# Eight of sixteen scan inputs made ahead on GpSimd, and one product with C per step on VectorE

## The chip, the cores and the metric

The kernel runs on one core of one Trainium2 chip. A time is the device time of one execution in microseconds (us). The profile names the engines PE (TensorE matmul), PEld (TensorE weight load), DVE (VectorE), ACT (ScalarE), POOL (GpSimd) and SP (SyncE, which here only issues DMAs).

## The reference, cut to what matters

Two layers follow each other. The part that matters is the state-space branch of the first layer's attention block: batch 2, length L = 1024, D = 128 channels, N = 128 states.

```python
xp = xn @ Wx                                   # xn: normed x
dr, Bs, Cs = xp[..., :R], xp[..., R:R + N], xp[..., R + N:]
delta = softplus(dr @ Wdt + bdt)               # dt
xn = xn * sel * gate                           # two sigmoid gates
Bs, Cs = Bs * imp, Cs * imp
def step(h, inputs):
    dt, bt, ct, xt = inputs
    dA = exp(dt[:, :, None] * A)
    h = dA * h + dt[:, :, None] * bt[:, None, :] * xt[:, :, None]
    y = sum(h * ct[:, None, :], axis=-1)
    return h, y
```

Beside it runs a softmax attention (16 heads of size 8, 4 key heads) on the same x; both are added, and an expert layer, a latent attention and a second expert layer follow.

## The kernel before, in words

The work stands in stages, each an `nc.Block` that all engines leave together.

`prepare` (0 to 66 us) makes dt (`delta`), B and C (`bt`, `ct`, states by time), and `gate`, which in the end holds dt times x. TensorE turns `bt` and `gate` so that time lies across partitions (`b_turned`, `x_turned`), and ScalarE copies them out. dt times x is also split into three bfloat16 parts (`parts`): `rest` and `low` on VectorE, casts on ScalarE. SP writes `delta`, `bt`, `ct` and the three parts to memory.

`hybrid_attention` (66 to 542 us) is the softmax attention: `HybridFront` first, then 16 half units. VectorE takes the maxima of scores in a pair of PSUM banks (L556); when a half unit's maxima are there it makes their parts in five small operations (L567 to L571). GpSimd meanwhile makes inputs of the later scan ahead of time (`gpsimd_third`, L734): B turned times one column of dt times x, 128x1024, and sends it to memory by a DMA of its own queue (L737), with two buffers. It takes six such products for each half unit, and waits for the half unit's `mparts_ready` before the next six. SP's `sync_third` reloads `ct`, `bt` and the parts near the end.

`scan_states` (542 to 1168 us) runs the recurrence for one channel at a time with the 128 states on partitions. A unit is one channel and one batch element, 128 states by 1024 times; 16 units make a step, 8 steps (jj) a batch element, and there are two of these (b): 256 units. For a unit n of a step:

- SP loads the channel's row of dt, broadcast to 128 partitions (`dt`, L1434, 512 KB), into one of four buffers; ScalarE makes the decay exp(dt A) from it (`da`, L1555).
- The input dt B x has to be in a PSUM pair. There are three ways. TURNED (units 0, 2, 4 to 14): ScalarE multiplies eight 128x128 tiles (`ut`, L1563) and TensorE transposes them (L1456). AHEAD_UNITS (3, 5, 7, 11, 13, 15): SP loads what GpSimd made (`ua`, L1432, three buffers) and TensorE transposes it (L1464). SPREAD (1 and 9): two matmuls of the bfloat16 parts spread dt times x to all partitions (L1470), and VectorE multiplies it with `bt` (L1590).
- VectorE runs the scan (L1598) from `da` in SBUF and the pair in PSUM into `st`; GpSimd multiplies `st` with `ct` into `hc` (L1639, two SBUF inputs); TensorE sums `hc` over the states with a one-column matmul (L1480, `reduce`) for four units at a time, when the fourth product is there.

There are three PSUM pairs for inputs, so the fill of unit n waits for the scan of an earlier unit (n - 3 for most), and four buffers each of `dt`, `da` and `st`. TensorE's order is written out by hand:

```python
for n in range(UNITS):
    if n % 2 == 1:
        jp, h = n // 4 - 1, (n % 4) // 2
        ...                      # reduce(b, jj, jp, h)
    if n + AHEAD < UNITS:
        fill(b, jj, n + AHEAD)   # AHEAD = 2
```

So at n = 9 TensorE first sums units 4 to 7, which needs the product of unit 7 (`hc_ready`), and only then fills unit 11. The same holds at n = 5, 13 and 1 for units 3, 11 and 15 of the four before.

In the text below a scan of unit n is Sn, a product of `st` with `ct` is Pn.

## Time and profile before

| | |
|---|---|
| median of 3 runs | 2047.4 us (2046.13 to 2053.39) |
| the profiled execution | 2043.78 us, span 2042.0 us |
| busy over the span | PE 86%, DVE 72%, ACT 65%, POOL 43% |
| granted TensorE clock, mean | 0.912 |
| prepare, attention, scan | to 65.7, to 542.4, to 1167.9 us (L1493 ends there) |
| the costliest groups | L1639 POOL 599.1 us, L1598 DVE 562.2 us, both in the scan |

Share of busy time is an average over stages with different limits; for this change the prepare, attention and scan stages are to be read apart. In a timeline row consecutive instructions of one line are merged: the first number is the start, the second the time to the end of the last of them, and xcount how many there are. In brackets stands the idle time ahead of it and what ended it.

### The profile page before, as it was taken

What the parts mean: (1) busy time and instruction counts of PE and PEld (TensorE: products, weight loads), DVE (VectorE), ACT (ScalarE), POOL (GpSimd) and SP (SyncE); (2) the same over time, 40 slices, a digit from 0 to 9 for tenths busy, and PEclk for the clock granted to TensorE, in tenths of its full rate; (3) what the DMA queues carried; (4) which work ended last, traced back from release to release, by engine and by line L of the source; (5) the groups of instructions that cost most, each with busy time, mean ns of one, the idle gap of its engine ahead of it and who ended that gap; (6) DMA issues with size and microseconds to landing.
All of it is one profiled execution on the core that took longest, in us unless ns stands there. A gap on an engine that the chain in (4) does not pass through costs nothing. (4 is left out here: it accounts for less than half of the span.)

```text
span 2042.0 us, 32184 instructions
## 1 busy us (share of the span) xinstructions
PE 1760.0 (86%) x10624; PEld 756.7 (37%) x10624; DVE 1467.8 (72%) x1473; ACT 1323.3 (65%) x2673; POOL 886.7 (43%) x567
## 2 busy tenths in 40 slices
PE   7769999999887776777777799899999998999996
PEld 2312333333344444444444333334444443233332
DVE  3677888887299999999999754556666624455456
ACT  4426777777799999989999534335555553554343
POOL 1075565565299999999999710000000001000000
PEclk8758999999998888988888899859999987999998
DMA  2354444442699888879888411322223000000000
GB/s 108 136 174 149 151 162 160 151 151 115 197 322 316 303 305 310 308 274 307 300 313 300 154 67 43 66 56 51 46 44 59 19 18 0 0 0 0 0 6 16
DMA packets 86546, 288.88 MB, mean 141 GB/s; under 512 B 11671, under 2 KB 15026, under 8 KB 84383
## 3 DMA queue, kind: packets, MB, share of 16 engines
q1 hardware_dynamic: 72319, 236.57, 36.4%
q0 software_dynamic: 13824, 50.34, 6.5%
q8 instruction: 71, 1.16, 0.2%
q10 hardware_dynamic: 288, 0.45, 0.1%
q14 instruction: 44, 0.36, 0.1%
HBM read 214.60 MB, written 61.21 MB: 135 GB/s over the span
## 5 line engine op out<-in xcount | busy, mean ns | idle before, releaser
L556 DVE TENSOR_REDUCE attn_mx<-banks 128x1 f32<-128x1024 f32 (+7 forms) x512 | 501.6, 989 | 156.2 <-PE banks L363 99.1
L1639 POOL TENSOR_TENSOR hc<-st,ct 128x1024 f32<-128x1024 f32 x256 | 599.1, 2387 | 6.0 <-DVE st L1598 5.6
L1598 DVE TENSOR_TENSOR_SCAN st<-da,banks 128x1024 f32<-128x1024 f32 x256 | 562.2, 2265 | 15.8 <-ACT da L1555 5.6
L508 ACT ACTIVATE attn_probs<-banks 128x512 f32<-128x512 f32 (+3 forms) x640 | 307.4, 533 | 199.0 <-PE banks L397 102.2
L1563 ACT ACTIVATE ut<-b_turned,mats 128x128 f32<-128x128 f32 x1024 | 311.7, 387 | 1.7
L1555 ACT ACTIVATE da<-dt,mats 128x1024 f32<-128x1024 f32 x256 | 282.3, 1138 | 25.4 <-DVE st L1598 21.3
L393 PE MATMUL banks<-attn_qa,attn_ka 75*128 75x512 bf16 (+3 forms) x896 | 272.5, 373 | 3.9 <-DMA attn_qa<-attn_mrow 2.0
L1480 PE MATMUL banks<-hc,onecol 128*32 128x512 f32 x1024 | 160.0, 701 | 105.3 <-POOL onecol L1637 77.2
L734 POOL TENSOR_TENSOR made_ahead<-b_turned,x_turned 128x1024 f32<-128x1024 f32 x96 | 183.9, 1915 | 116.8 <-DVE attn_mparts L571 74.4
L361 PE MATMUL banks<-attn_ka,attn_qa 64*128 64x512 bf16 (+3 forms) x512 | 199.7, 391 | 34.2 <-DVE attn_mx L556 26.5
L413 PE MATMUL banks<-attn_probs,attn_vst 128*32 128x256 f32 (+3 forms) x2560 | 191.1, 369 | 1.7 <-ACT attn_osb L499 1.4
L1456 PE MATMUL banks<-mats,ut 128*128 128x128 f32 x1024 | 165.6, 301 | 30.5 <-DVE st L1598 19.8
L508 ACT ACTIVATE centred_squares<-banks 128x512 f32<-128x512 f32 x256 | 138.9, 594 | 62.5 <-PE banks L393 61.1
L1456 PEld LDWEIGHTS banks<-mats,ut 128*128 128x128 f32 x1024 | 134.7, 153 | 64.5 <-ACT ut L1563 35.1
L2574 PE MATMUL banks<-hid_m,ew 128*128 128x512 f32 x320 | 157.4, 627 | 0.0
L3011 POOL CAST route_ident<-mats 128x128 bf16<-128x128 f32 x1 | 0.3, 292 | 345.6 <-issue 345.6
L361 PE MATMUL banks<-attn_ku,attn_qu 64*128 64x512 bf16 (+3 forms) x384 | 145.7, 380 | 0.0
L1464 PEld LDWEIGHTS banks<-mats,ua 128*128 128x128 f32 x768 | 105.8, 169 | 107.1 <-issue 71.5
L1464 PE MATMUL banks<-mats,ua 128*128 128x128 f32 x768 | 132.2, 328 | 6.5 <-DVE st L1598 6.4
L393 PEld LDWEIGHTS banks<-attn_qa,attn_ka 75*128 75x128 bf16 x896 | 80.8, 98 | 132.6 <-issue 48.5
L361 PEld LDWEIGHTS banks<-attn_ka,attn_qa 64*128 64x128 bf16 x512 | 47.9, 94 | 207.0 <-issue 126.8
L413 PE MATMUL banks<-centred_squares,attn_vst 128*32 128x256 f32 x1024 | 83.1, 396 | 2.2 <-ACT attn_osb L499 2.2
(438 smaller groups left out, 1949.0 us busy)
## 6 DMA issues: line engine op xcount, KB each, us to landing
dt<-dt_rows SPq DMA_DIRECT2D x256, 512.0 KB, 5.6
ahead<-made_ahead POOLq DMA_DIRECT2D x96, 512.0 KB, 3.1
ua<-ahead SPq DMA_DIRECT2D x96, 512.0 KB, 5.8
attn_qa<-q_lin SPq DMA_DIRECT2D x144, 64.0 KB
attn_qu<-attn_qa SPq DMA_DIRECT2D x16, 512.0 KB, 4.3
attn_ka<-k_lin SPq DMA_DIRECT2D x72, 64.0 KB
moe_w<-in_moe_w SPq DMA_DIRECT2D x2, 2048.0 KB, 10.2
mats<-in_mats SPq DMA_DIRECT2D x1, 2876.5 KB, 12.9
```

What stands on the lines that cost most here:

```text
L361: ins = nc.tensor.matmul(out[:, lo:hi], lhs, rhs, start=True, stop=not diag)
L393: ins = nc.tensor.matmul(out[:, c0:BLK], ka[i % RING][0:KROWS, kj(j), sl(kt, TILE)], qa[i % RING][0:KROWS, j, qb * BLK + c0:(qb + 1) * BLK ...
L413: last = nc.tensor.matmul(out_acc[32 * j:32 * j + 32, cols], vstage[:, kt, kj(j), :], probs[(kt_slot + j // 2) % 4][:, j % 2, cols],  star ...
L508: nc.scalar.activation(probs[s % 4][:, jj, c0:BLK], scores_exp[jj][:, c0:BLK], ACT.Exp, scale=scale).then_inc(probs_ready, 1)
L556: nc.vector.reduce_max(mx[:, qt, j:j + 1], scores_max[n % 2][:, 0:w], AX.X)\
L734: nc.gpsimd.tensor_tensor(stage[:, :, :], scan.b_turned[:, 8 * b:8 * b + 8, :], x, ALU.mult)\
L1456: ins = nc.tensor.transpose(pair[:, i // 4, sl(i % 4, TILE)], buf[:, i, :], k.m("ident"))
L1464: ins = nc.tensor.transpose(pair[:, i // 4, sl(i % 4, TILE)], ua[q % 3][:, i, :], k.m("ident"))
L1555: nc.scalar.activation(da[n % 4][:, :], dt[n % 4][:, :], ACT.Exp, scale=a_now[:, g, jp:jp + 1])\
L1563: nc.scalar.activation(ut[TURNED.index(n) % 2][:, i, :], b_turned[:, 8 * b + i, :], ACT.Copy, scale=x_now[:, i, g, jp:jp + 1]).then_inc(ut ...
L1598: nc.vector.tensor_tensor_scan(st[n % 4][:, :], da[n % 4][:, :], pair[:, :, :].rearrange("p h t -> p (h t)"), 0.0, ALU.mult, ALU.add).then ...
L1639: nc.gpsimd.tensor_tensor(hc[n % 8][:, :], st[n % 4][:, :], ct[:, b * SEQ:(b + 1) * SEQ], ALU.mult)\
```

## The change

It makes five edits.

1. `AHEAD_UNITS` has eight units (2, 4, 6, 8, 10, 12, 14, 15) where it had six. GpSimd makes 128 products ahead where it made 96, eight for each half unit of the attention. `ua` has four buffers where it had three.
2. SPREAD is gone. TURNED is 0, 1, 3, 5, 7, 9, 11, 13, still eight units. VectorE makes no input any more.
3. The product of `st` with `ct` for unit 8 of each step goes from GpSimd to VectorE (`ON_DVE`); VectorE waits for its own scan and for `summed`, then multiplies. GpSimd passes over the unit.
4. With the spread its parts fall away: `rest`, `low`, eight casts, the `sel` table, and the writes and reloads of `bt` and the parts (one write of 1024 KB and three of 512 KB; one load of 1024 KB and twelve of 128 KB).
5. `bt` lives only until the end of the attention; the attention's own bfloat16 parts of q and k, which used the scan's `xparts` buffer, get one of their own.

```diff
         self.rs_tok = k.sb("rs_tok", [128, NT], ctx=ctx)
-        self.qparts = [scan.xparts[:, i, :] for i in range(3)]
-        self.kparts = [scan.xparts[:, 3, sl(i)] for i in range(3)]
+        parts = k.sb("qk_parts", [128, 4, T], BF16, ctx)
+        self.qparts = [parts[:, i, :] for i in range(3)]
+        self.kparts = [parts[:, 3, sl(i)] for i in range(3)]
         self.stage = [k.sb(f"made_ahead{i}", [128, SEQ // TILE, TILE], ctx=ctx) for i in range(2)]
...
         sp.dma_start(self.scan.ct[:, :], self.d["ct_kept"]).then_inc(self.scan_in, 16)
-        sp.dma_start(self.scan.bt[:, :], self.d["bt_kept"]).then_inc(self.scan_in, 16)
-        for p in range(3):
-            for g in range(4):
-                sp.dma_start(self.scan.xparts[32 * p:32 * p + 32, g, :], self.d["xparts_kept"][p, sl(g, 32), :])\
-                    .then_inc(self.scan_in, 16)
-        sp.wait_ge(self.scan_in, 16 * 14)
+        sp.wait_ge(self.scan_in, 16)
...
                 for m in AHEAD_UNITS:
-                    if n >= 7 and n % 6 == 1:
-                        pool.wait_ge(self.mparts_ready[(n // 6 - 1) % 2], (n // 6 + 1) // 2)
+                    if n >= 9 and n % 8 == 1:
+                        pool.wait_ge(self.mparts_ready[(n // 8 - 1) % 2], (n // 8 + 1) // 2)
                     channel = 32 * (m % 4) + 4 * jj + m // 4
...
         self.kept = kept
-        self.bt = k.sb("bt", [128, T], ctx=ctx)
         self.ct = k.sb("ct", [128, T], ctx=ctx)
         self.b_turned = k.sb("b_turned", [128, NT, 128], ctx=ctx)
         self.x_turned = k.sb("x_turned", [128, NT, 128], ctx=ctx)
-        self.xparts = k.sb("xparts", [128, 4, T], BF16, ctx)
-        self.sel = k.sb("sel", [96, 32], BF16, ctx)
         self.a_neg = k.m("A_log")
 
 
-AHEAD_UNITS = [3, 5, 7, 11, 13, 15]
+AHEAD_UNITS = [2, 4, 6, 8, 10, 12, 14, 15]
 
 
 def hybrid_attention(k, d, scan, rall, sqc, ssm_in, attn_t):
...
-            for b in range(NB):
-                act.wait_ge(dtx_ready, b + 1)
-                nc.scalar.copy(parts[0][:, sl(b)], gate[:, sl(b)]).then_inc(high_ready, 1)
-                if b == 0:
-                    continue
-                out = ready("bturn", b - 1)
-                nc.scalar.copy(b_turned[:, sl(b - 1, 4), :].rearrange("p t m -> p (t m)"), out[:, :])\
-                    .then_inc(b_copied, 1)
-            out = ready("bturn", NB - 1)
-            nc.scalar.copy(b_turned[:, sl(NB - 1, 4), :].rearrange("p t m -> p (t m)"), out[:, :]).then_inc(b_copied, 1)
-            for b in range(NB):
-                act.wait_ge(rest_ready, b + 1)
-                nc.scalar.copy(parts[1][:, sl(b)], log1[:, sl(b)]).then_inc(middle_ready, 1)
-                out = ready("xturn", b)
-                nc.scalar.copy(x_turned[:, sl(b, 4), :].rearrange("p t m -> p (t m)"), out[:, :]).then_inc(x_copied, 1)
+            for what, dst, copied in (("bturn", b_turned, b_copied), ("xturn", x_turned, x_copied)):
+                for b in range(NB):
+                    out = ready(what, b)
+                    nc.scalar.copy(dst[:, sl(b, 4), :].rearrange("p t m -> p (t m)"), out[:, :]).then_inc(copied, 1)
...
             input_of(3)
-            for b in range(NB):
-                rest(b)
-            for b in range(NB):
-                low(b)
...
                 sp.dma_start(d["dt_rows"][:, sl(h, SEQ)], delta[:, sl(h, SEQ)]).then_inc(sent, 16)
-            for ready, buf, kept in ((bt_ready, bt, "bt_kept"), (ct_ready, ct, "ct_kept")):
-                sp.wait_ge(ready, NB)
-                sp.dma_start(d[kept], buf[:, :]).then_inc(sent, 16)
-            for p, ready in enumerate((high_ready, middle_ready, low_ready)):
-                sp.wait_ge(ready, NB)
-                sp.dma_start(d["xparts_kept"][p], parts[p][:, :]).then_inc(sent, 16)
-            sp.wait_ge(sent, 16 * 7)
+            sp.wait_ge(ct_ready, NB)
+            sp.dma_start(d["ct_kept"], ct[:, :]).then_inc(sent, 16)
+            sp.wait_ge(sent, 16 * 3)
 
...
     zero = k.m("Wdt")
-    SPREAD = [1, 9]
-    TURNED = [n for n in range(16) if n not in SPREAD + AHEAD_UNITS]
+    TURNED = [n for n in range(16) if n not in AHEAD_UNITS]
+    ON_DVE = 8
     NA = len(AHEAD_UNITS)
     PAIR = [1, 2, 3, 1, 2, 3, 1, 2, 3, 1, 2, 3, 1, 2, 3, 2]
...
-    ua = [k.sb(f"ua{i}", [128, 8, 128], ctx=ctx) for i in range(3)]
+    ua = [k.sb(f"ua{i}", [128, 8, 128], ctx=ctx) for i in range(4)]
...
+    def by_pool(s, n):
+
+        return (UNITS - 1) * s + n - (1 if n > ON_DVE else 0)
...
-                    after(sp, ua_turned, place - 2, place, 3)
+                    after(sp, ua_turned, place - 3, place, 4)
                     source = ahead[bass.ds(NA * (jj + STEPS * b) + q, 1)].rearrange("n p t m -> (n p) t m")
-                    sp.dma_start(ua[q % 3][:, :, :], source).then_inc(ua_arrived[q % 3], 16)
+                    sp.dma_start(ua[q % 4][:, :, :], source).then_inc(ua_arrived[q % 4], 16)
...
-                    return
-                w = sel[:, bass.ds(4 * jj + n // 4, 1)].to_broadcast([96, 128])
-                for h in range(2):
-                    cols = slice(b * SEQ + h * BLK, b * SEQ + (h + 1) * BLK)
-                    last = nc.tensor.matmul(pair[:, h, :], w, xparts[0:96, n % 4, cols], start=True, stop=True)
-                last.then_inc(dtx_spread, 1)
+                q = AHEAD_UNITS.index(n)
+                pe.wait_ge(ua_arrived[q % 4], 16 * (NA // 4 * s + q // 4 + 1))
+                for i in range(8):
+                    ins = nc.tensor.transpose(pair[:, i // 4, sl(i % 4, TILE)], ua[q % 4][:, i, :], k.m("ident"))
+                ins.then_inc(ua_turned, 1)
...
-                    pe.wait_ge(hc_ready, UNITS * s + 4 * jp + 4)
+                    pe.wait_ge(hc_ready, by_pool(s, 4 * jp + 4))
+                    if jp == ON_DVE // 4:
+                        pe.wait_ge(hc_on_dve, s + 1)
...
-                if n in SPREAD:
-                    made = spread_index(b, jj, n) + 1
-                    dve.wait_ge(dtx_spread, made)
-                    b_rows = bt[:, b * SEQ:(b + 1) * SEQ].rearrange("p (h t) -> p h t", h=2)
-                    nc.vector.tensor_tensor(pair[:, :, :], b_rows, pair[:, :, :], ALU.mult).then_inc(input_ready, 1)
-                    dve.wait_ge(input_ready, made)
-                elif n in AHEAD_UNITS:
+                if n in AHEAD_UNITS:
                     dve.wait_ge(ua_turned, NA * s + AHEAD_UNITS.index(n) + 1)
                 else:
                     dve.wait_ge(ut_turned, turned_index(b, jj, n) + 1)
                 dve.wait_ge(decay_ready, u + 1)
-                after(dve, hc_ready, u - 3, u, 4)
+                after(dve, hc_ready, by_pool(s, n - 3), u, 4)
+                if n == ON_DVE + 4:
+                    dve.wait_ge(hc_on_dve, s + 1)
                 nc.vector.tensor_tensor_scan(st[n % 4][:, :], da[n % 4][:, :],
                                              pair[:, :, :].rearrange("p h t -> p (h t)"), 0.0,
                                              ALU.mult, ALU.add).then_inc(state_ready, 1)
+                if n == ON_DVE:
+                    dve.wait_ge(state_ready, u + 1)
+                    dve.wait_ge(summed, 4 * s + n // 4 - 1)
+                    nc.vector.tensor_tensor(hc[n % 8][:, :], st[n % 4][:, :], ct[:, b * SEQ:(b + 1) * SEQ], ALU.mult)\
+                        .then_inc(hc_on_dve, 1)
 
             def take_sums(b):
 
@@ -1635,6 +1586,8 @@
                     after(pool, summed, 4 * s + jp - 1, u, 8)
...
                     nc.gpsimd.tensor_copy(col[jp % 2][:, :], one_at_j).then_inc(col_ready, 1)
+                if n == ON_DVE:
+                    return
                 pool.wait_ge(state_ready, u + 1)
                 nc.gpsimd.tensor_tensor(hc[n % 8][:, :], st[n % 4][:, :], ct[:, b * SEQ:(b + 1) * SEQ], ALU.mult)\
                     .then_inc(hc_ready, 1)
...
                     rall = k.sb("norms", [128, BLK], ctx=normed)
+                    scan.bt = k.sb("bt", [128, T], ctx=normed)
                     sqc = [k.sb(f"centred_squares{i}", [128, 2, BLK], ctx=normed) for i in range(2)]
```

Lines of the rows below are those of each kernel's own file: L1598 of before is L1544 after, L1590 falls away, L1550 is the new product.

On VectorE, this is the first step of the scan before, from its first unit; `banks_3`, `banks_5` and `banks_7` are the three PSUM pairs, and the order view names the scan SCALAR_TENSOR_TENSOR:

```order
L1598 SCALAR_TENSOR_TENSOR st<-da,banks_3 128x1024
L1590 TENSOR_TENSOR banks_5<-bt,banks_5 128x1024
L1598 SCALAR_TENSOR_TENSOR st<-da,banks_5 128x1024
L1598 SCALAR_TENSOR_TENSOR st<-da,banks_7 128x1024
L1598 SCALAR_TENSOR_TENSOR st<-da,banks_3 128x1024
L1598 SCALAR_TENSOR_TENSOR st<-da,banks_5 128x1024
L1598 SCALAR_TENSOR_TENSOR st<-da,banks_7 128x1024
L1598 SCALAR_TENSOR_TENSOR st<-da,banks_3 128x1024
L1598 SCALAR_TENSOR_TENSOR st<-da,banks_5 128x1024
L1598 SCALAR_TENSOR_TENSOR st<-da,banks_7 128x1024
L1590 TENSOR_TENSOR banks_3<-bt,banks_3 128x1024
L1598 SCALAR_TENSOR_TENSOR st<-da,banks_3 128x1024
```

And this is the same engine in the changed kernel, from unit 3 to unit 11 of that step:

```order
L1544 SCALAR_TENSOR_TENSOR st<-da,banks_3 128x1024
L1544 SCALAR_TENSOR_TENSOR st<-da,banks_5 128x1024
L1544 SCALAR_TENSOR_TENSOR st<-da,banks_7 128x1024
L1544 SCALAR_TENSOR_TENSOR st<-da,banks_3 128x1024
L1544 SCALAR_TENSOR_TENSOR st<-da,banks_5 128x1024
L1544 SCALAR_TENSOR_TENSOR st<-da,banks_7 128x1024
L1550 TENSOR_TENSOR hc<-st,ct 128x1024
L1544 SCALAR_TENSOR_TENSOR st<-da,banks_3 128x1024
L1544 SCALAR_TENSOR_TENSOR st<-da,banks_5 128x1024
L1544 SCALAR_TENSOR_TENSOR st<-da,banks_7 128x1024
```

The two multiplies ahead of units 1 and 9 are gone, and one multiply of two SBUF tensors stands behind unit 8.

On TensorE, this is what stands before from the fill of unit 9 to the fill of unit 12 in the first step (the row with `scan_hc_ready` is the sum of units 4 to 7):

```order
L1470 MATMUL banks_3<-xparts,sel 128x512 [waits scan_state_ready]
L1470 MATMUL banks_3<-xparts,sel 128x512
L1456 MATMUL banks_5<-mats,ut 128x128 [waits scan_ut_ready,scan_state_ready]
L1456 MATMUL banks_5<-mats,ut 128x128 [waits scan_ut_ready] x7
L1480 MATMUL banks_1<-hc,onecol 32x512 [waits scan_hc_ready,scan_col_ready]
L1480 MATMUL banks_1<-hc,onecol 32x512 x3
L1464 MATMUL banks_7<-mats,ua 128x128 [waits scan_ua_arrived0,scan_state_ready]
L1464 MATMUL banks_7<-mats,ua 128x128 x7
L1456 MATMUL banks_3<-mats,ut 128x128 [waits scan_ut_ready,scan_state_ready]
L1456 MATMUL banks_3<-mats,ut 128x128 [waits scan_ut_ready] x7
```

And the same place in the changed kernel:

```order
L1411 MATMUL banks_3<-mats,ut 128x128 [waits scan_ut_ready,scan_state_ready]
L1411 MATMUL banks_3<-mats,ut 128x128 [waits scan_ut_ready] x7
L1418 MATMUL banks_5<-mats,ua 128x128 [waits scan_ua_arrived0,scan_state_ready]
L1418 MATMUL banks_5<-mats,ua 128x128 x7
L1430 MATMUL banks_1<-hc,onecol 32x512 [waits scan_hc_ready,scan_col_ready]
L1430 MATMUL banks_1<-hc,onecol 32x512 x3
L1411 MATMUL banks_7<-mats,ut 128x128 [waits scan_ut_ready,scan_state_ready]
L1411 MATMUL banks_7<-mats,ut 128x128 [waits scan_ut_ready] x7
L1418 MATMUL banks_3<-mats,ua 128x128 [waits scan_ua_arrived1,scan_state_ready]
L1418 MATMUL banks_3<-mats,ua 128x128 x7
```

The fill of unit 9 becomes eight transposes in place of two matmuls, and units 10 to 12 change their source; the sum of units 4 to 7 still stands ahead of the fill of unit 11.

## Rows read from the trace of the kernel before

**Rows 1.** Windows: us, busy time by engine (x instructions), granted clock, DMA share, GB/s.

```profile
200.00:300.00 100.00, 98.75 (x832) 33.35 (x828) 83.86 (x96) 73.66 (x141) 61.88 (x51) 1.00 0.45 154
900.00:1100.00 200.00, 147.24 (x961) 88.49 (x963) 197.54 (x96) 191.73 (x439) 199.88 (x107) 0.86 0.89 305
915.00:921.00 6.00, 5.36 (x24) 3.51 (x24) 5.81 (x4) 5.65 (x15) 6.00 (x5) 0.50 0.82 251
```

**Rows 2.** Timeline of DVE in one step of the scan.

```profile
914.13 1.21 DVE L1590 TENSOR_TENSOR banks<-bt,banks 128x1024 f32<-128x1024 f32 x1
915.53 17.53 DVE L1598 TENSOR_TENSOR_SCAN st<-da,banks 128x1024 f32<-128x1024 f32 x8 [0.19 <-POOL hc L1639]
```

**Rows 3.** Timeline of POOL in the same step.

```profile
905.99 0.23 POOL L1637 COPY onecol<-mats 128x32 f32 x1
906.15 9.34 POOL L1639 TENSOR_TENSOR hc<-st,ct 128x1024 f32<-128x1024 f32 x4
915.41 0.23 POOL L1637 COPY onecol<-mats 128x32 f32 x1
```

**Rows 4.** Timeline of ACT: the copy that opens a step.

```profile
618.27 0.29 ACT L1546 COPY mats<-x_turned 128x128 f32 x1
654.81 0.29 ACT L1546 COPY mats<-x_turned 128x128 f32 x1
```

**Rows 5.** Timeline of PE round unit 9 of that step.

```profile
912.18 1.14 PE L1456 MATMUL banks<-mats,ut 128*128 128x128 f32 x8 [1.47 <-DVE st L1598]
915.64 1.93 PE L1480 MATMUL banks<-hc,onecol 128*32 128x512 f32 x8 [2.33 <-POOL onecol L1637]
917.50 1.97 PE L1464 MATMUL banks<-mats,ua 128*128 128x128 f32 x8
```

**Rows 6.** Timeline of prepare's end and the attention's first row.

```profile
54.90 0.33 SPq L1347 DMA_DIRECT2D ct_kept<-ct  x1
55.42 1.91 PE L1180 MATMUL banks<-mats,gate 128*128 128x128 f32 x16
56.38 5.55 SPq L1350 DMA_DIRECT2D xparts_kept<-xparts_lin  x3
60.89 0.69 DVE L1306 TENSOR_TENSOR xparts_lin<-log,xparts_lin 128x512 bf16<-128x512 f32 x1 [0.31 <-ACT xparts_lin L1249]
65.70 0.33 SPq L691 DMA_DIRECT2D bt<-in_rope_q  x1
```

**Rows 7.** The page's DMA issues: KB each, median us to landing.

```profile
bt_kept<-bt SPq DMA_DIRECT2D x1, 1024.0 KB, 3.9
ct_kept<-ct SPq DMA_DIRECT2D x1, 1024.0 KB, 6.8
```

**Rows 8.** Timeline of DVE and POOL together, in three places.

```profile
127.85 1.92 POOL L734 TENSOR_TENSOR made_ahead<-b_turned,x_turned 128x1024 f32<-128x1024 f32 x1
128.70 1.11 DVE L567 TENSOR_SCALAR attn_mneg<-attn_mx 128x16 f32<-128x16 f32 x1
...
309.63 0.17 DVE L567 TENSOR_SCALAR attn_mneg<-attn_mx 128x16 f32<-128x16 f32 x1
...
51.67 1.27 POOL L1338 TENSOR_TENSOR gate<-gate,xg 128x512 f32<-128x512 f32 x1 [6.43 <-ACT gate L1236]
52.98 0.69 DVE L1294 TENSOR_TENSOR gate<-gate,delta 128x512 f32<-128x512 f32 x1 [0.93 <-POOL gate L1338]
53.39 1.42 POOL L1338 TENSOR_TENSOR gate<-gate,xg 128x512 f32<-128x512 f32 x1 [0.44 <-ACT gate L1236]
```

**Rows 9.** POOL's timeline late in the attention; its waits, 190 to 500 us.

```profile
482.84 1.90 POOL L734 TENSOR_TENSOR made_ahead<-b_turned,x_turned 128x1024 f32<-128x1024 f32 x1 [7.36 <-DVE attn_mparts L571]
...
485.66 1.93 POOL L734 TENSOR_TENSOR made_ahead<-b_turned,x_turned 128x1024 f32<-128x1024 f32 x1
...
POOL made_ahead L734 <- DVE attn_mparts L571: 56.4, 12, 7.4
POOL made_ahead L734 <- DMA ahead<-made_ahead: 35.5, 23, 4.0
```

More of the change, by code:

```diff
@@ L1077, in prepare @@
     bt, ct, b_turned, x_turned = scan.bt, scan.ct, scan.b_turned, scan.x_turned
-    sel, a_neg = scan.sel, scan.a_neg
+    a_neg = scan.a_neg
     y0 = k.sb("prep_guess", [128, BLK], ctx=ctx)
@@ L1094, in prepare @@
     dr = k.sb("dr", [R_DT + 1, T], ctx=ctx)
-    parts = [k.sb(f"xparts_lin{i}", [128, T], BF16, ctx) for i in range(3)]
     bsg = k.sb("bsg", [128, 1], ctx=ctx)
@@ L1114, in prepare @@
     dtx_ready = k.sem("prep_dtx")
-    high_ready = k.sem("prep_high")
-    rest_ready = k.sem("prep_rest")
-    middle_ready = k.sem("prep_middle")
-    low_ready = k.sem("prep_low")
     b_copied = k.sem("prep_b_copied")
@@ L1295, in input_of @@
                     .then_inc(dtx_ready, 1)
-            def rest(b):
-                dve.wait_ge(high_ready, b + 1)
-                dve.wait_ge(dtx_ready, b + 1)
-                nc.vector.tensor_tensor(log1[:, sl(b)], gate[:, sl(b)], parts[0][:, sl(b)], ALU.subtract)\
-                    .then_inc(rest_ready, 1)
-            def low(b):
-                dve.wait_ge(middle_ready, b + 1)
-                dve.wait_ge(rest_ready, b + 1)
-                nc.vector.tensor_tensor(parts[2][:, sl(b)], log1[:, sl(b)], parts[1][:, sl(b)], ALU.subtract)\
-                    .then_inc(low_ready, 1)
             gated(0)
@@ L1332, in _ @@
             pool.wait_ge(tables, 1)
-            nc.gpsimd.tensor_copy(sel[:, :], k.m("eye96", 96)).then_inc(tables, 1)
-            pool.wait_ge(tables, 2)
             for b in range(NB):
@@ L1365, in scan_states @@
     nc = k.nc
-    bt, ct, b_turned, x_turned, xparts = scan.bt, scan.ct, scan.b_turned, scan.x_turned, scan.xparts
-    sel, a_neg = scan.sel, scan.a_neg
+    ct, b_turned, x_turned = scan.ct, scan.b_turned, scan.x_turned
+    a_neg = scan.a_neg
     free = k.m("Wx")
@@ L1389, in scan_states @@
     ut_turned = k.sem("scan_ut_turned")
-    ua_arrived = [k.sem(f"scan_ua_arrived{i}") for i in range(3)]
+    ua_arrived = [k.sem(f"scan_ua_arrived{i}") for i in range(4)]
     ua_turned = k.sem("scan_ua_turned")
-    dtx_spread = k.sem("scan_dtx_spread")
     decay_ready = k.sem("scan_decay_ready")
-    input_ready = k.sem("scan_input_ready")
     state_ready = k.sem("scan_state_ready")
     hc_ready = k.sem("scan_hc_ready")
+    hc_on_dve = k.sem("scan_hc_on_dve")
     summed = k.sem("scan_summed")
@@ L1459, in fill @@
                     return
-                if n in AHEAD_UNITS:
-                    q = AHEAD_UNITS.index(n)
-                    pe.wait_ge(ua_arrived[q % 3], 16 * (NA // 3 * s + q // 3 + 1))
-                    for i in range(8):
-                        ins = nc.tensor.transpose(pair[:, i // 4, sl(i % 4, TILE)], ua[q % 3][:, i, :], k.m("ident"))
-                    ins.then_inc(ua_turned, 1)
-                    return
-                w = sel[:, bass.ds(4 * jj + n // 4, 1)].to_broadcast([96, 128])
-                for h in range(2):
-                    cols = slice(b * SEQ + h * BLK, b * SEQ + (h + 1) * BLK)
-                    last = nc.tensor.matmul(pair[:, h, :], w, xparts[0:96, n % 4, cols], start=True, stop=True)
-                last.then_inc(dtx_spread, 1)
+                q = AHEAD_UNITS.index(n)
[3 more added lines that the diff above has]
+                ins.then_inc(ua_turned, 1)
             def reduce(b, jj, jp, h):
@@ L3051, in build_program @@
         rest_in = k.sem("weights_arrived")
-        for name in ("bt", "ct"):
-            scratch[f"{name}_kept"] = nc.dram_tensor(f"{name}_kept", [128, T], F32, kind="Internal").ap()
-        scratch["xparts_kept"] = nc.dram_tensor("xparts_kept", [3, 128, T], BF16, kind="Internal").ap()
+        scratch["ct_kept"] = nc.dram_tensor("ct_kept", [128, T], F32, kind="Internal").ap()
         scratch["ahead"] = nc.dram_tensor("ahead", [T // SEQ * D // 16 * len(AHEAD_UNITS), 128, SEQ // TILE, TILE], F32,
```

2 lines of the change are left out of this document (removed).

## The prediction

> **What bounds the kernel now.** I read the window view first, to see which engine has no idle time in which stage. In the attention it is PE: 98.75 us of 100, with DVE at 83.9 and POOL at 61.9. In the scan POOL is busy for 199.9 of 200 us and DVE for 197.5, ACT for 191.7, PE for 147; the DMA share is 0.89 [rows 1]. So the scan runs at the pace of two engines at once, and the timelines say at which. POOL makes four products and a column copy in 915.41 - 905.99 = 9.42 us, so a step of 16 units is 37.7 us; the copy costs 0.16, a product 2.315 [rows 3]. On DVE an input multiply stands from 914.13 to the next scan's start at 915.53, 1.40 us with a wait of 0.19 on its own result; half a step is 18.84, so eight scans take 17.44 and one 2.18 us from start to start; the eight rows end 17.53 after the first start, so a scan by itself lasts 2.26 [rows 2]. That is 34.9 + 2.8 = 37.7: both engines are full. ACT can do a step in 36.5 us: that is what it took while it was catching up early in the stage [rows 4].
>
> **The change, part by part.**
>
> *Prepare.* The block ends when the last of the three part writes has landed: it is issued when `low` of block 3 is done (60.89 + 0.69 = 61.6), and the attention's first row is at 65.70 [rows 6]. Afterwards two things are left: the copies behind the last turn, which ends at 57.3, and the write of `ct`, issued at 54.9. `bt`'s write, the same size with none ahead of it, took 3.9 us to land, and `ct`'s behind it 6.8 [rows 7]: it lands at 58.8 to 61.7. With 0.4 for leaving the block (my allowance; before, issue, landing and leaving took 4.1 together), the attention starts at 59.2 to 62.1, 3.6 to 6.5 us earlier. I take 6, since the write then goes alone. The reloads at the attention's end lie beside its last half unit: nothing.
>
> *Attention.* POOL makes 32 more products. One costs 485.66 - 482.84 = 2.82 us with its issue. A half unit now has six (16.9 us), a mean wait of 56.4 / 12 = 4.7 us for `mparts`, and 35.5 / 12 = 3.0 us of waits for its own writes: 24.6 us [rows 9]. Eight take 22.6, with the same 3.0 us 25.6. So POOL goes from waiting to being about 1 us per half unit late. It is late for nobody directly: behind its last wait, which ended at 482.8, stand five products before and seven now, 19.7 us, and if it slips by 1 us for each of 15 half units as well it is done near 518; the stage ends at 542. But POOL is no longer idle when DVE makes the parts, and there is a row for what that does: L567, 0.17 us at 309.63 where POOL was waiting, took 1.11 us at 128.70, and it ended at 129.81, when the POOL product that ran since 127.85 ended (129.77) [rows 8]. Such a DVE instruction was held until POOL's had ended. With POOL in a product for 1.9 of 2.82 us, a late POOL meets DVE in two of three half units and holds it for half a product, 0.95 us. PE has another PSUM pair to fill meanwhile, so I let only a fifth of it through: 12 half units x 0.67 x 0.95 x 0.2, about 2 us with rounding up; bounds 0 and 8.
>
> *The scan's start.* The load of unit 2's input now stands ahead of the first dt row in SP's queue, and unit 1's input has to be made by ACT: 0.7 us, from 0 to 2.
>
> *The scan's steps, added up by engine.* DVE: 34.9 + 0.19 wait + 1.1 (the new product at the L1590 row's 1.21, less the overlap with the next scan) = 36.2. POOL: 15 x 2.315 + 4 x 0.16 = 35.4. ACT keeps eight inputs and 16 decays: 36.5. PE gets two fills of eight transposes for two of two matmuls; a fill took 1.14 us [rows 5], so at most 2.3 us a step, and PE is idle for a quarter, 10 us. DMA gets 24 loads of 512 KB for 22: 0.89 x 24 / 22 = 0.97 of the time at the same pace, 1.00 at 36.6 us. By sums alone a step would fall by about 1 us. What decides is how the steps interlock.
>
> *POOL's delay at unit 7.* POOL's product takes 2.315 and the scan 2.18, so POOL falls behind by 0.135 us a unit and 0.16 at each column. It is level at unit 9 (it skips 8 and has to wait for S9). Fourteen units later P7 starts 0.08 + 14 x 0.135 + 3 x 0.16 = 2.45 us after the end of S7, that is 0.27 after the end of S8. DVE asks for its product at 0.19 after S8. So the new product meets POOL at the change from P6 to P7, within a tenth of a microsecond.
>
> *Two SBUF inputs on both.* Both products read two SBUF tensors. For that pair the trace has one overlap: `gate` times `delta` on DVE from 52.98 to 53.67, and POOL's product started at 53.39 took 1.42 where the one before took 1.27 [rows 8]. With L567 I read this as: one of the two waits for the other. Then there are two orders. (a) P7 is first: DVE waits for it. The loop from P9 to P9 is 14 x 2.315 + 3 x 0.16 = 32.9 to P7's start, 2.25 for P7, 1.2 for the DVE product, 2.26 for S9 and 0.08: 38.6 us. (b) DVE is first: P7 ends 1.15 later, near the end of S9. PE sums units 4 to 7 before it fills unit 11, so both come behind P7; in the row for that place they took 1.93 and 1.97 us, since PE had waited 1.47 and 2.33 us and the granted clock was 0.50 (1.2 GHz) [rows 5, 1]. S11 then starts 3.9 us after P7's end, not 2.2. The loop from P11 to P11 is 12 x 2.315 + 3 x 0.16 + 2.3 + 1.2 (DVE) + 3.9 + 2.26 + 0.2 = 38.1 us. Steps of both kinds will mix: 38.4. That is 0.7 us more than 37.7, for 14 steps; the first step and the one at the change of the batch element have pauses of their own in which POOL gets level, and are left at about -1.5 together. Sum of the steps: 14 x 0.7 - 1.5 = +8.3.
>
> The Trainium skill, SBUF — State Buffer, section "Who interferes with whom", states this as a rule: a VectorE instruction with two SBUF inputs contends with a GpSimd instruction that reads SBUF, whoever is first has the shared ports for its whole instruction, and the other is fully blocked. By it the scan, with one SBUF input, and the old multiply with `bt`, the other operand in PSUM, are free of it, and the new product is not; the trace agrees in that L1598 lies beside POOL's products at 2.26 us each time. By the rule the step is 38.4; without it, by the rival below, 36.9.
>
> **Sum.** -6 (prepare) + 2 (attention) + 0.7 (start) + 8.3 (steps) = +5.0 us against the profiled execution's 2043.8, so 2048.8. That execution is 3.6 us below the median of the runs, 2047.4; on the median it is 2052.4, and I say 2052.
>
> **Rivals.**
>
> *The two products don't hold each other.* For it: the only pair of two-input products overlapped by 0.28 us and cost 0.15, and L567 is another operation with one input. Then P7 runs from 0.27 to 2.6 after S8 beside DVE's product. The loop by PE is 12 x 2.315 + 0.5 + 2.3 + 3.9 + 2.26 + 0.2 = 36.9 at the slow clock, the floor is ACT's 36.5 and DMA's 36.6. With 36.9: 14 x -0.8 = -11, -1.5 for the two pauses, -6, +2 and +0.7: -16, about 2031; with 36.5 2025, with DMA or ACT stalls of 0.4 us in each step 2037.
>
> *The scan stays at 37.7.* DVE's other short waits spread out, POOL gets level in between and the meeting costs about the 1.5 us that DVE's sum won (37.7 less 36.2). Then prepare, attention and start count, -6 + 2 + 0.7, and 1 for the pauses: -4, 2043. Against it: in (a) the loop is a chain of POOL instructions, which waits of DVE elsewhere don't shorten until they sum to over 2 us.
>
> *Slower.* POOL holds DVE in the attention and PE has no slack for it. PE is at 98.75%, so it decides there once the hold is over what the second pair covers, roughly 1 us a half unit; at 1 us in each of 12 half units, not 2 but 12, and with the rest 2062. Against it: DVE is busy for only 84 of 100 us and can catch up. No row shows PE's slack. The same sum comes out if all steps are of kind (a) and unit 7's fill is late too (39.1 each).
>
> **Chances.** The forecast, +2 to +9 us, 0.45; not held, 0.30; scan unchanged, 0.10; slower by over 10, 0.15. What can be told from no change is about 0.5%, 10.2 us. Faster takes the second case without its weak end and a little of the third: 0.31. Slower takes the last and the forecast's edge: 0.20. Same: 0.49. The range reaches from the good end of the gain, 2025, to the slower case, 2062; the forecast's own is 2048 to 2058.
>
> **What the profile afterwards would show.** Right: L1550 with a mean well over 1.21 us (up to 3.5) or DVE waits ahead of it; POOL about 0.93 busy in the scan, not 1.00; a scan stage of over 620 us to its last L1488 or L1493 row; steps of 38.1 to 38.6 us between two L1546 copies of ACT; L567 over 0.17 us in most half units; the attention's first row near 60. Wrong: L1550 at 1.2 us beside a running POOL product, steps under 37.2 us, ACT or DMA as the last to wait for.

## The result

The changed kernel takes 2076.2 us (median of 7 runs, 2062.1 to 2081.5), the kernel before 2050.6 in its 7 runs; the ratio is 1.0118, 95% interval [1.0086, 1.0149]. It is slower by 1.2%, 14 us beyond the upper end of the range. The profiled execution took 2079.8 us (span 2078.0) against 2043.8. The three boundaries between the stages first: the first row of the attention, the fill that opens the scan, and the one that opens the layer behind it (it is the first operation of that layer's attention code).

```profile
63.30 0.34 SPq L692 DMA_DIRECT2D bt<-in_rope_q  x1
...
557.97 0.17 DVE L1530 MEMSET mats<- 128x128 f32 x1 [4.93 <-PEq L261]
...
1196.98 0.94 POOL L326 MEMSET attn_ones<- 3x1024 bf16 x1 [7.29 <-POOLq L1375]
```

Before, these are 65.7 [rows 6], 542.5 and 1169.6. So prepare became 2.4 us shorter, the attention 17.9 longer (494.7 for 476.8), the scan 12.0 longer (639.0 for 627.0), and the rest of the program, which has the same code, 8.5 longer (881.0 for 872.4). The forecast had -6, +2, +9 and 0.

Windows of the changed kernel, beside [rows 1]:

```profile
200.00:300.00 100.00, 93.08 (x766) 29.76 (x760) 85.99 (x87) 68.37 (x129) 78.25 (x63) 0.97 0.54 188
900.00:1100.00 200.00, 145.27 (x995) 91.86 (x992) 192.69 (x88) 185.38 (x420) 186.78 (x97) 0.89 0.91 323
```

PE, which had 98.75 us of 100, has 93.1; POOL went from 61.9 to 78.3. In the scan no engine is full any more: POOL is at 0.93, DVE at 0.96. Where the attention lost it, DVE and POOL between 233 and 242 us, and PE behind them:

```profile
235.81 0.17 DVE L567 TENSOR_SCALAR attn_mneg<-attn_mx 128x16 f32<-128x16 f32 x1
236.02 2.48 DVE L568 CAST attn_mparts<-attn_mneg 128x16 bf16<-128x16 f32 x1
238.53 0.18 DVE L569 TENSOR_TENSOR attn_mres<-attn_mneg,attn_mparts 128x16 f32<-128x16 f32 x1
238.74 0.17 DVE L570 CAST attn_mparts<-attn_mres 128x16 bf16<-128x16 f32 x1
238.95 2.38 DVE L571 TENSOR_TENSOR attn_mparts<-attn_mres,attn_mparts 128x16 bf16<-128x16 f32 x1
```

```profile
235.91 0.59 POOL L733 DMA_DIRECT2D ahead<-made_ahead  x1 [0.30 <-POOL made_ahead L730]
236.53 1.92 POOL L730 TENSOR_TENSOR made_ahead<-b_turned,x_turned 128x1024 f32<-128x1024 f32 x1
238.75 0.59 POOL L733 DMA_DIRECT2D ahead<-made_ahead  x1 [0.30 <-POOL made_ahead L730]
239.36 1.92 POOL L730 TENSOR_TENSOR made_ahead<-b_turned,x_turned 128x1024 f32<-128x1024 f32 x1
```

```profile
241.38 0.48 PE L374 MATMUL banks<-attn_identb,attn_mparts 128*12 128x128 bf16 x3 [3.48 <-DVE attn_mparts L571]
```

Five chained operations that take 1.0 us together took 5.5: L568 ended at 238.50, as POOL's product did (238.45), and L571 at 241.33, as the next product did (241.28). PE then waited 3.48 us, and ran at a granted clock of 0.50 (1.2 GHz) from 242 to 246:

```profile
242.00:246.00 4.00, 4.00 (x23) 0.68 (x16) 2.92 (x4) 1.66 (x3) 3.66 (x4) 0.50 0.45 179
```

That half unit took about 6 us more than 24.6. Over the whole stage, before and after in the windows view, and then the row on this wait for L571, which in the view of before is one wait of 1.4 us:

```profile
65.70:542.50 476.80, 444.56 (x3418) 148.04 (x3418) 358.84 (x413) 309.95 (x582) 250.11 (x204) 0.93 0.43 145
63.30:558.00 494.70, 451.58 (x3418) 147.72 (x3418) 377.23 (x414) 310.46 (x582) 330.35 (x268) 0.91 0.48 168
...
PE banks L374 <- DVE attn_mparts L571: 10.3, 6, 3.5
```

PE does the same 3418 matmuls. It is idle for 43.1 us instead of 32.2 (10.9 more), and busy for 7.0 us more, at a granted clock of 0.91 instead of 0.93.

In the scan, a step of the changed kernel, DVE and then POOL, beside [rows 2, 3]:

```profile
773.13 4.44 DVE L1544 TENSOR_TENSOR_SCAN st<-da,banks 128x1024 f32<-128x1024 f32 x2
777.70 3.57 DVE L1550 TENSOR_TENSOR hc<-st,ct 128x1024 f32<-128x1024 f32 x1
781.20 6.63 DVE L1544 TENSOR_TENSOR_SCAN st<-da,banks 128x1024 f32<-128x1024 f32 x3
```

```profile
770.83 9.34 POOL L1592 TENSOR_TENSOR hc<-st,ct 128x1024 f32<-128x1024 f32 x4
780.10 1.24 POOL L1588 COPY onecol<-mats 128x32 f32 x1
783.55 7.01 POOL L1592 TENSOR_TENSOR hc<-st,ct 128x1024 f32<-128x1024 f32 x3 [2.21 <-DVE st L1544]
```

DVE's product of unit 8 asks at 777.70 and is held until POOL's product of unit 7 ends at 780.17; then it runs its 1.1 us, and POOL's column copy, 0.23 us otherwise, is held meanwhile (1.24). Only then comes scan 9, for which POOL's product of unit 9 waits. From the end of POOL's product 7 to the start of its product 9 pass 3.38 us. Steps are 38.7 us, before 37.7.

### The profile page after: what moved, and what is told of

The parts are those of the page before. It is cut to its first block and busy times, and to the rows that moved or that the text cites. A ratio compares the mean times of both kernels' runs of the same rounds, so it can differ in the third digit from the quotient of the medians.

```text
span 2078.0 us, 32583 instructions
## 1 busy us (share of the span) xinstructions
PE 1779.0 (86%) x10816; PEld 775.4 (37%) x10816; DVE 1483.2 (71%) x1449; ACT 1321.8 (64%) x2665; POOL 946.4 (46%) x614
## 5 line engine op out<-in xcount | busy, mean ns | idle before, releaser
L556 DVE TENSOR_REDUCE attn_mx<-banks 128x1 f32<-128x1024 f32 (+7 forms) x512 | 501.0, 990 | 156.5 <-PE banks L363 100.3
L1544 DVE TENSOR_TENSOR_SCAN st<-da,banks 128x1024 f32<-128x1024 f32 x256 | 562.1, 2262 | 25.5 <-PE banks L1411 17.0
L1592 POOL TENSOR_TENSOR hc<-st,ct 128x1024 f32<-128x1024 f32 x240 | 560.8, 2372 | 40.0 <-DVE st L1544 39.9
L730 POOL TENSOR_TENSOR made_ahead<-b_turned,x_turned 128x1024 f32<-128x1024 f32 x128 | 245.2, 1915 | 47.9 <-DMA ahead<-made_ahead 40.7
L1430 PE MATMUL banks<-hc,onecol 128*32 128x512 f32 x1024 | 155.5, 683 | 117.2 <-POOL hc L1592 100.5
L1418 PE MATMUL banks<-mats,ua 128*128 128x128 f32 x1024 | 154.8, 301 | 35.3 <-DVE st L1544 31.9
L1418 PEld LDWEIGHTS banks<-mats,ua 128*128 128x128 f32 x1024 | 129.5, 156 | 65.3 <-DVE st L1544 59.7
L393 PEld LDWEIGHTS banks<-attn_qa,attn_ka 75*128 75x128 bf16 x896 | 80.5, 98 | 133.2 <-issue 52.0
L733 POOL DMA_DIRECT2D ahead<-made_ahead x128 | 76.3, 596 | 40.8 <-POOL made_ahead L730 37.7
```

The costliest lines, as they stand in the source:

```text
L393: ins = nc.tensor.matmul(out[:, c0:BLK], ka[i % RING][0:KROWS, kj(j), sl(kt, TILE)], qa[i % RING][0:KROWS, j, qb * BLK + c0:(qb + 1) * BLK ...
L556: nc.vector.reduce_max(mx[:, qt, j:j + 1], scores_max[n % 2][:, 0:w], AX.X)\
L730: nc.gpsimd.tensor_tensor(stage[:, :, :], scan.b_turned[:, 8 * b:8 * b + 8, :], x, ALU.mult)\
L1418: ins = nc.tensor.transpose(pair[:, i // 4, sl(i % 4, TILE)], ua[q % 4][:, i, :], k.m("ident"))
L1544: nc.vector.tensor_tensor_scan(st[n % 4][:, :], da[n % 4][:, :], pair[:, :, :].rearrange("p h t -> p (h t)"), 0.0, ALU.mult, ALU.add).then ...
L1592: nc.gpsimd.tensor_tensor(hc[n % 8][:, :], st[n % 4][:, :], ct[:, b * SEQ:(b + 1) * SEQ], ALU.mult)\
```

## The experiments

Ten more kernels were run, and the two given ones once more. The table has for each profiled execution the time at which the attention begins, the stages as cut above, and the sum of the durations of L567 to L571 over the first attention's 16 half units (14.0 us if nothing holds them).

| kernel | begins | attention | L567-L571 | scan | rest | ratio to before, 95% |
|---|---|---|---|---|---|---|
| before | 65.7 | 476.8 | 14.9 | 627.0 | 872.4 | |
| before, again | 67.4 | 476.0 | 15.2 | 628.1 | 884.6 | |
| changed | 63.3 | 494.7 | 34.2 | 639.0 | 881.0 | 1.0118 [1.0086, 1.0149] |
| changed, again | 59.5 | 486.9 | 31.6 | 640.6 | 872.2 | 1.0098 [1.0069, 1.0127] |
| extra_made | 65.7 | 492.5 | 34.8 | 627.5 | 882.3 | 1.0087 [1.0061, 1.0112] |
| six_made | 59.2 | 474.5 | 14.7 | 640.5 | 878.3 | 1.0036 [1.0018, 1.0054] |
| sent_not_made | 59.2 | 477.7 | 14.0 | 639.7 | 875.3 | 1.0044 [1.0028, 1.0059] |
| product_later | 60.9 | 488.7 | 32.5 | 616.2 | 886.4 | 1.0039 [1.0016, 1.0062] |
| sent_later | 65.0 | 484.1 | 18.7 | 639.5 | 881.4 | 1.0047 [1.0025, 1.0070] |
| both_mended | 62.4 | 478.5 | 20.0 | 617.0 | 885.6 | 0.9962 [0.9939, 0.9985] |
| all_on_pool | 61.8 | 495.3 | 35.6 | 625.1 | 874.0 | 1.0043 [1.0023, 1.0064] |
| two_on_dve | 61.1 | 488.9 | 32.3 | 654.5 | 885.2 | 1.0186 [1.0146, 1.0226] |
| state_in_psum | 59.3 | 502.7 | 35.7 | 621.9 | 878.3 | 1.0049 [1.0029, 1.0070] |
| both_psum | 60.9 | 479.4 | 20.8 | 621.3 | 872.2 | 0.9971 [0.9951, 0.9990] |

### The attention's part alone: extra_made

The kernel before, with two more products for every six.

```diff
-                for m in AHEAD_UNITS:
-                    if n >= 7 and n % 6 == 1:
-                        pool.wait_ge(self.mparts_ready[(n // 6 - 1) % 2], (n // 6 + 1) // 2)
+                for m in AHEAD_UNITS + EXTRA:
+                    if n >= 9 and n % 8 == 1:
+                        pool.wait_ge(self.mparts_ready[(n // 8 - 1) % 2], (n // 8 + 1) // 2)
```

> The kernel before, its scan untouched, in which GpSimd makes and sends two more products for every six in the first attention (128 instead of 96, with the changed kernel's rule of eight per half unit; the 32 more go to rows that nobody reads). Theory (a GpSimd product in flight holds VectorE's small operations of the maxima, and TensorE waits behind them): the attention goes from 476.7 to about 494 us, the means of L567 to L571 rise well over 0.17 us, the scan stays 627, the ratio is about 1.009. Rival A (the attention's 18 us came from the moved buffers or from the clock, not from GpSimd): attention within 4 us of 477. The other rival (transfers in each other's way) also gives 494 here, and is told apart by the run that sends without making.

Attention 492.5, scan 627.5, ratio 1.0087: the attention's loss comes with the 32 more products and their transfers, without the moved buffers and without the new scan.

### The scan's part alone: six_made

```diff
-                for m in AHEAD_UNITS:
+                for m in AHEAD_UNITS[0:6]:
...
-                    source = ahead[bass.ds(NA * (jj + STEPS * b) + q, 1)]
+                    source = ahead[bass.ds(6 * (jj + STEPS * b) + q % 6, 1)]
```

with the old gate at every sixth product. Two of each eight products are not made, and the scan reads two others in their place.

> The changed kernel, but only the first six of each eight products are made ahead, under the old rule of six per half unit; in the scan units 14 and 15 read the products of the first two units in their place (so the products of these two units are left out of the output). Theory: attention back to 477 us (within 3), prepare stays 63, the scan stays at 639, so the time is that of before plus 10: ratio 1.005. Rival (the scan's 12 us more come from the products made late, or from the pressure that the attention leaves): the scan falls to under 632.

Attention 474.5, scan 640.5: each of the two losses is had without the other.

### Products or transfers: sent_not_made

The changed kernel leaves out seven eighths of each product, and sends the whole buffer.

```diff
-                    nc.gpsimd.tensor_tensor(stage[:, :, :], scan.b_turned[:, 8 * b:8 * b + 8, :], x, ALU.mult)
+                    nc.gpsimd.tensor_tensor(stage[:, 0:1, :], scan.b_turned[:, 8 * b:8 * b + 1, :], x[:, 0:1, :],
+                                            ALU.mult)
```

> The changed kernel, but GpSimd makes only one eighth of each product ahead (128 of its 1,024 columns), and sends the whole 0.5 MB buffer as before (seven eighths of the products are left out of the output). Theory (held by GpSimd's product): attention falls to 477 us or a little under, since an operation of 0.3 us holds nobody for long; L567 to L571 come back to 0.17 us nearly always; scan unchanged at 639; ratio 1.005 or less. Rival (the 32 transfers more, or GpSimd's issues of them, are what costs): attention stays over 490 us.

All 128 transfers of 512 KB are still there, and the attention is 477.7. L567 in the first attention, every one of 16 at 174 or 175 ns:

```profile
L567 DVE TENSOR_SCALAR attn_mneg<-attn_mx x16: 174/174/175, 122.5 to 500.5; 128x16 f32<-128x16 f32 x16
```

The transfers cost 3 us at most (477.7 beside the 474.5 of six_made); what costs is POOL's time in products. (With products of 0.39 us POOL was also through long before the next maxima, so this run doesn't tell whether so short a product would hold.)

### The scan's order: product_later and two_on_dve

```diff
-                if n == ON_DVE:
-                    dve.wait_ge(state_ready, u + 1)
+                if n == ON_DVE + 1:
+                    dve.wait_ge(state_ready, u)
                     dve.wait_ge(summed, 4 * s + n // 4 - 1)
-                    nc.vector.tensor_tensor(hc[n % 8][:, :], st[n % 4][:, :], ct[...], ALU.mult)
+                    nc.vector.tensor_tensor(hc[ON_DVE % 8][:, :], st[ON_DVE % 4][:, :], ct[...], ALU.mult)
```

> The changed kernel with one move: VectorE makes the product of unit 8 after the scan of unit 9, not straight after the scan of unit 8. Theory (in each step GpSimd is 2 to 3 us late at unit 8, so VectorE's product is held until GpSimd's product of unit 7 ends): one scan later (2.19 us) that product has nearly ended and GpSimd waits for scan 9 anyway, so L1550's mean falls from 2.2 to 1.2 to 1.6 us and a step from 38.7 to 37.1 to 37.8: the scan stage 612 to 625 us instead of 639, attention unchanged at 494; ratio to before about 1.004. Rival 1 (the hold is there wherever GpSimd is working, at random): L1550 stays at 2.2 and the scan at 639. Rival 2 (GpSimd's product of unit 9, released by the same scan, gets in first): L1550 near 3.5 in every step, and the scan over 645.

The scan stage fell by 23 us to 616.2, 11 less than before the change; steps of 36.4 to 37.5. The product (duration min, median, max), and one step on DVE and on POOL:

```profile
L1550 DVE TENSOR_TENSOR hc<-st,ct x16: 1198/1199/1493, 579.0 to 1139.6; 128x1024 f32<-128x1024 f32 x16
```

```profile
720.15 6.64 DVE L1544 TENSOR_TENSOR_SCAN st<-da,banks 128x1024 f32<-128x1024 f32 x3 [1.03 <-PE banks L1411]
726.71 1.20 DVE L1550 TENSOR_TENSOR hc<-st,ct 128x1024 f32<-128x1024 f32 x1
```

```profile
716.48 9.34 POOL L1592 TENSOR_TENSOR hc<-st,ct 128x1024 f32<-128x1024 f32 x4
725.78 0.20 POOL L1588 COPY onecol<-mats 128x32 f32 x1
726.87 8.00 POOL L1592 TENSOR_TENSOR hc<-st,ct 128x1024 f32<-128x1024 f32 x3 [0.89 <-DVE st L1544]
```

POOL's product 7 ends at 725.82, scan 9 at 726.8, and DVE gets its product in first. POOL's product 9 starts at 726.87 and is held beside it: three products took 8.00 us, not 7.0. From POOL's product 7 to the real start of its product 9 it is 2.0 us instead of 3.4. The same product, one scan later, turns a loss of 12 us into a gain of 11.

The other way round, a second product straight after its own scan:

```diff
-    ON_DVE = 8
+    ON_DVE = [0, 8]
```

> The changed kernel with two products with C per step on VectorE, those of units 0 and 8, and 14 on GpSimd. Theory (the hold is GpSimd's lag at that point, about 0.14 us per unit of 2.19, and 0.2 per small copy): with the second product GpSimd has 14 x 2.33 + 0.9 = 33.5 us of work against 35.1 of scans and catches up twice a step, so each product is held 1.2 us and less instead of 2.2, L1550's mean falls to 1.3 to 1.9 us, and a step takes 35.1 + 2 x 1.3 to 1.9 = 37.7 to 38.9, that is no more than with one product: scan stage 625 to 642. Rival (each product of VectorE costs what the first did, 3.5 us with its hold): steps of over 41, scan over 680.

Both theories missed: 654.5, steps of 39.6. The products took 2.23 us in the median, 1.0 of it held. What fits, worked out afterwards, is POOL's own chain. Each product that DVE makes straight after its scan is held until POOL's product ends, and gives POOL a pause of 3.38 us from there (DVE's product and the next scan), however long the hold was; in this trace the pauses near 760 and 780 us are 3.36. With one: 15 x 2.315 + 4 x 0.16 + 3.38 = 38.7 (measured 38.7). With two: 14 x 2.315 + 4 x 0.16 + 2 x 3.38 = 39.8 (39.6). It also says why L1550 varied from 1.3 to 3.6 us in the changed kernel while its steps did not vary.

### All products on POOL: all_on_pool

```diff
-                if n == ON_DVE:
-                    return
```

and VectorE's product with its waits taken out.

> The changed kernel with the product of unit 8 given back to GpSimd, so that it makes all 16 products in the scan and VectorE none. Theory: no hold in the scan; GpSimd's 16 products of 2.33 us and four small copies bound the step as in the kernel before: steps of 37.7, scan stage 626 to 629 us; attention 488 to 495. So the 12 us of the scan stage are the one product's, and dropping the spread units bought the scan nothing. Rival (without the 32 multiplications of PSUM on VectorE per batch the scan has become shorter by itself, rival (i) of the prediction): steps under 37.

Scan 625.1, with steps from 36.5 to 39.3. So the hold and its pause are all of the scan's loss, and dropping the spread units alone gives 2 to 3 us at most. The rival with steps under 37 holds for some steps and not for the stage.

### What the hold needs: state_in_psum

The order of the changed kernel, but scan 8 writes in place into PSUM and DVE's product reads the state there.

```diff
+                state = pair[:, :, :].rearrange("p h t -> p (h t)") if n == ON_DVE else st[n % 4][:, :]
-                nc.vector.tensor_tensor_scan(st[n % 4][:, :], da[n % 4][:, :],
+                nc.vector.tensor_tensor_scan(state, da[n % 4][:, :],
...
-                    nc.vector.tensor_tensor(hc[n % 8][:, :], st[n % 4][:, :], ct[...], ALU.mult)
+                    nc.vector.tensor_tensor(hc[n % 8][:, :], state, ct[...], ALU.mult)
```

> The changed kernel, its order kept, but the scan of unit 8 writes its state in place into PSUM, and VectorE's product of it reads one operand there and only C from SBUF (the computation is the same; TensorE's refill for unit 11 waits for the product). Theory A (the hold needs both operands of VectorE's product in SBUF; the scans and the maxima, which read PSUM, run at 2.2 and 1.2 us beside GpSimd throughout): L1553's mean 1.2 to 1.3 instead of 2.37, and GpSimd's copies beside it stay at 0.23; GpSimd's wait for scan 9 shrinks to what the product itself takes, so steps of 36.5 to 37.7 and a scan stage of 616 to 628. Theory B (one operand in SBUF is enough for a hold): L1553 as before 1.3 to 3.6, steps 38.7, scan 639. Attention 488 to 495 in both.

```profile
L1553 DVE TENSOR_TENSOR hc<-banks,ct x16: 1224/1224/1225, 590.2 to 1156.2; 128x1024 f32<-128x1024 f32 x16
```

```profile
739.03 1.22 DVE L1553 TENSOR_TENSOR hc<-banks,ct 128x1024 f32<-128x1024 f32 x1
```

```profile
732.05 9.37 POOL L1595 TENSOR_TENSOR hc<-st,ct 128x1024 f32<-128x1024 f32 x4
741.35 0.22 POOL L1591 COPY onecol<-mats 128x32 f32 x1
```

DVE's product lies wholly inside POOL's product 7, which ends at 741.42, and neither takes longer: 16 of 16 within 1 ns of 1.224 us, scan 621.9. POOL's next product starts at 742.52, so its pause is 1.1 us and not 3.4. With one operand in PSUM nothing is held. (The attention drew 502.7 in this trace, the most of all; its code is the changed kernel's.)

### The attention mended: sent_later, both_mended, both_psum

A third buffer in the dead rope tables, and a product is sent after the next one has been issued:

```diff
-                    pool.wait_ge(self.made_ahead, n + 1)
-                    pool.dma_start(self.d["ahead"][n], stage[:, :, :]).then_inc(kept, 16)
+                    if n > 0:
+                        self.send_made(pool, n - 1)
```

> The changed kernel with GpSimd's loop ahead made shorter: three buffers (the third in the dead rope tables), and each product is sent after the next one has been issued, so that GpSimd no longer waits 0.3 us for its own product nor for a buffer. Eight products then take about 8 x (1.92 + 0.6) = 20.2 us instead of 22.7 and more, of the 24.6 us of a half unit, and the gate at every eighth product holds GpSimd back until VectorE's five operations are past. All 128 products and transfers are still there. Theory: L567 to L571 are back at 0.17 us in nearly all half units, attention at 477 to 480 us instead of 494.6, scan 639: ratio to before 1.004 (prepare -6, scan +12, the rest drawn by the clock). Rival (32 products more cost TensorE or VectorE through sheer activity, whichever way they lie): attention stays over 488.

> The changed kernel with both moves: GpSimd's shorter loop ahead, and VectorE's product of unit 8 after the scan of unit 9. Nothing is left out. Theory: prepare -5 to -6, attention within 3 of before's 476.7, scan 616 (as in the run with the later product alone) against 627.1: sum -17 to -14, less what the rest of the program draws by the clock (up to +14 in the runs so far): ratio 0.992 to 0.998, faster than both kernels. Rival (the two moves take from each other): ratio over 1.0.

> State in PSUM as in the run before it, and GpSimd's shorter loop ahead in the attention (three buffers, sent later). Theory A: attention 477 to 484, scan 616 to 628, ratio 0.995 to 1.0, that is close to the kernel with the later product (0.996). Theory B: scan 639, ratio 1.004 as in the run with the shorter loop alone.

With this loop alone the five operations are at 18.7 us and the attention at 484.1, more than the 480 expected (its profiled execution, 2071.85 us, is one of the two longest of 12 with a median of 2058.2, and had a granted clock of 0.92 in the attention); with the later product too it is 478.5, with the state in PSUM 479.4. Windows of both_mended:

```profile
200.00:300.00 100.00, 98.75 (x830) 32.69 (x829) 84.86 (x94) 74.18 (x141) 80.46 (x65) 1.00 0.58 201
900.00:1100.00 200.00, 152.37 (x1037) 97.14 (x1037) 194.09 (x93) 193.39 (x440) 195.48 (x103) 0.87 0.93 338
```

PE is back at 98.75 with POOL busier than in the changed kernel (80.5): it is not how much POOL works but whether it is in a product when DVE combines the maxima. both_mended takes 2043.1 us beside 2050.0 for the kernel before: 0.4% faster, with an interval that ends below 1.

### Both kernels once more

> The kernel before once more, for a second trace. If the 8.5 us by which the rest of the program (behind the scan) was longer in the changed kernel's trace are a draw of the clock, this trace has another length there than 872.4 us, between 872 and 886 as in the ten traces so far, with attention 477 and scan 627 within 1 us. If the change lengthens the rest, it is 872 again. And the attention begins between 59 + 6 and 65 + 6 us, or at 65.7 again.

> The changed kernel once more. Scan 639 within 1 us, attention 489 to 496 (which products hold VectorE is drawn anew), the attention's beginning 59 to 65 us, the rest 874 to 886: a draw, not the change. Ratio to before 1.010 to 1.014.

The rest of the program is 884.6 in this trace of the kernel before and 872.2 in this one of the changed kernel: opposite to the first pair. Over the 14 traces it goes from 872.4 to 884.6 in the three with the old scan and from 872.2 to 886.4 in the others. The 8.5 us are a draw. It goes with the granted clock of the stage, which is 0.94 in the three traces of 872 us and 0.92 in the four of over 884; no run set the clock. Of what was expected of the changed kernel, the attention (486.9), the scan (640.6), the rest and the ratio (1.0098) came out just beyond their ranges.

## Why the prediction was wrong

**Prepare, -6.** Right in size, but not in the first trace (-2.4). The attention begins at 59.2 to 65.0 in the 11 traces with the change, 61.1 on average, and at 65.7 to 67.4 in the three without, 66.3: -5.2.

**Attention, +2: the step that failed.** The forecast saw the mechanism in [rows 8] and mis-sized it; it is +10 to +18 in the changed kernel's two traces, +16 on average over the seven traces with the full loop ahead. That POOL would be late and still be done near 518 us was right: its last product ended at 518.2. It had "12 half units x 0.67 x 0.95 x 0.2", 12 holds of L567 with a fifth let through. Of its factors, two fell. First, the held time: 34.2 - 14.0 = 20 us, not 7.6. L567 alone gave 9.4 us in 10 holds, near the 7.6 forecast; the other four operations of the chain, which the forecast left out, gave 10.9, nearly all of it in five holds of over 2 us. Second, the fifth: in those seven traces the sum of the five operations is 33.8 us on average, 18.8 more than in the two traces of the kernel before, and PE is idle for 42.2 us, 10.8 more. So nearly six tenths of the held time come through as idle time of PE. The second PSUM pair did not cover it: PE waits for L571's result, and DVE, which is behind the hold, also empties the pairs that PE fills (a reading of the rows; no run changed the pairs). The other 5.6 of the 16.4 us are busy time of PE, 450.6 us for 445.0 with the same matmuls at a granted clock of 0.90 to 0.93, before 0.93. The forecast had no term for that. At 242 us the low clock follows a hold; how much of the 5.6 us the holds cause stays open, since sent_later, with few holds, has 448.5 us too. The rival "Slower" had the right mechanism ("PE has no slack for it") and was priced at 12 of attention and 2062 in all; it was given 0.15.

**Scan, +9: right, a little small.** It came to +12. Start and kind (a) were as described: the chain of POOL's instructions gives 38.6 in the forecast (its terms add up to 38.7), 38.7 measured. The term that was off is the mix: "Steps of both kinds will mix: 38.4" did not happen: 14 of the 16 products of DVE were held, by 0.6 us or more, so the steady steps cost 1.0 us each, not 0.7. The two rivals on this side fell: the two products do hold each other, and the scan did not stay at 37.7. The forecast did not look at what makes (a) dear: the pause of POOL is DVE's product plus a whole scan, so the place of the product in DVE's order decides. That is why the run that only moves it gains.

**The rest, 0.** The two profiled executions are 36 us apart and the medians of all runs 25.6. Prepare, attention and scan give -5.2 + 16.4 + 12.3 = +23.5 (the scan: 639.9 on average in the five traces with its changed code, 627.5 in the three with its old one).

**The rule.** The Trainium skill, SBUF — State Buffer, section "Who interferes with whom", was weighed for DVE's product alone. The runs agree with it there, both ways: held with two SBUF inputs (1.3 to 3.6 us), free with one in PSUM (1.224 us, 16 of 16). The same section says that copies, casts and `tensor_scalar` can enter the modes that take the shared ports, and that a `tensor_tensor` with both inputs in SBUF contends: that names L567 to L571, all five. The 256 maxima (L556), which read PSUM and which it exempts, have a mean of 1,222 ns before and after. Reading it for the chain, and not for the one new instruction, would have put all five operations into the sum; how often each meets a product it does not say.

## What to carry to other kernels

- More work on an engine with idle time is not free if it shares something with the bound engine's supplier. Look at every short VectorE operation on SBUF that the bound engine waits for, not only at the longest, and when that engine is as full as PE is here (98.75 of 100 us), price a hold at well over half its length.
- Idle time can be a fence. The old gate left POOL waiting when DVE combined the maxima (one hold in 16 half units); the new one let it run on. Keep the gap (a shorter loop, or a gate in front of the sensitive place) or put one operand into PSUM (run here for the scan's product alone, not for the five operations).
- In two coupled engines, a product placed one instruction later on DVE was worth 23 us of 639: put it where the other engine would wait anyway.
